# A fused attention, SwiGLU and layer-norm kernel: ScalarE's first tanh placed between two pairs of q copies

## The chip, the cores and the metric

The kernel runs on one core of a Trainium2 chip. The time is the device time of one execution in microseconds (us); lower is better. PE is TensorE, ACT is ScalarE, DVE is VectorE, POOL is GpSimd, and SP issues the DMAs.

## The reference, cut to what matters

There are 64 sequences of 64 tokens with 256 features. Everything is float32.

```
x = x + a_alpha * attention(gamma_a * rmsnorm(x) + beta_a)      # 16 heads of 16
x = x + f_alpha * (silu(h @ gate_w.T) * (h @ hidden_w.T) @ out_w.T + out_b)
                                                                # h = gamma_f * rmsnorm(x) + beta_f, 1024 hidden columns
y = (layernorm(x) * weight + bias + tanh(cond @ lin_w.T + lin_b)) * weight + bias
```

Each gamma, beta and alpha is a product of the sequence's condition vector (64 numbers) with a table. `silu(u)` is computed as `0.5 * u * (1 + tanh(u / 2))`, so each gate block needs one tanh on ACT.

## The kernel before, in words

The 64 sequences are cut into 8 groups (`GROUPS`) of 8 sequences, that is 512 tokens. The work is a software pipeline that is written out by hand as one instruction list for each engine: `head(g)` makes keys, values and queries of group g and finishes group g-2, and `main(g)` does the attention of group g together with the feed-forward part of the group before it, f = g-1. On each engine `head(1)`, `main(1)` and `head(2)` are written out, a hardware loop runs `main(i)`, `head(i + 1)` for i = 2 to 6, and `main(7)` and the end are written out again. So `head` with a group before it occurs seven times, for g = 1 to 7. Engines meet only through semaphores. Matrix products in float32 are done as three products of a high and a low part: six matmuls of 128x512 for one 128-column block with its 256 inputs.

The feed-forward part has 8 blocks c of 128 hidden columns. For each, PE makes a gate block and a hidden block (`gate_hidden`, L593, 12 matmuls). ACT applies tanh to the gate block in PSUM bank 2 and writes `act_t` (`tanh`, L778). DVE makes (tanh + 1) * gate (L1106), which frees bank 2, and then multiplies by half of the hidden block in bank 3 (L1110, which frees bank 3). ACT copies the result to `hs` as its high part (`hidden_hi`, L785), and POOL makes the low part (L1288). PE multiplies both with the output weights (`ffn_out`, L616). Bank 2 is the only gate bank in `main`, so the gate block c+1 waits until DVE's L1106 of block c is done (L580, semaphore `h_steps`).

For block 0, PE does four gate and four hidden matmuls first, then the last two of the gate and the last two of the hidden block, since those last ones need the low part that POOL makes of the normed input (`x2s`, L1273).

The change touches the place where `head(g)` hands over to `main(g)`. PE ends `head(g)` with the q projection (`q_proj`, L418) into banks 4 and 5. These two banks are read by two engines: DVE makes `qpar` (`q_out`, L1037, four instructions, first two of bank 4 and then two of bank 5), and ACT makes `qpair` (`pair_q`, L749, four instructions, first two of bank 5, h = 1, and then two of bank 4, h = 0). Each engine waits for the other's first pair before it goes on to the second (`qpair_ready`, `q_ready`), so that they do not read one bank together.

PE's `main(g)` goes on with `gate_hidden(f, 0)`, `scores_for_max(g, 0)`, `scores_for_max(g, 1)` (L478, eight matmuls each), `gate_hidden(f, 1)`, `ffn_out(f, 0)` and so on. `scores_for_max(g, 0)` writes banks 6 and 7. `scores_for_max(g, 1)` writes banks 4 and 5, where q lies, so it first waits for all four `qpar` and all four `qpair` copies:

```
                if n == 1 and later(g):
                    pe.wait_ge(q_ready, 4 * g + 4)
                    pe.wait_ge(qpair_ready, 4 * g + 4)
```

ACT's order before is `pair_q(g)` at the end of `head(g)`, then at the start of `main(g)` `feed(f, 0)`, which is `tanh(f, 0)` and `hidden_hi(f, 0)`, then two copies that place v (L763), then `feed(f, 1)`.

Of the kernel before, what the change touches and what calls it, by code (L numbers as in the profile page):

```python
# [88 lines left out]
def build(nc, x, condT, tabT, linT, linb, lnw, lnb, wqkT, wvT, woT, ghT, outT, outb_dram,  # L89
          consts, out):  # L90
    with ExitStack() as ctx:
# [124 lines left out]
        def later(g):  # L216

            return not isinstance(g, int) or g > 0
# [498 lines left out]
        def _(act):  # L717
            def cut_hi(n):
                act.wait_ge(ld_stage[n], 16)
                nc.scalar.activation(chunks[n][1], stage_view(n), ACT.Copy).then_inc(stage_hi, 1)  # L720
# [6 lines left out]
            def xs_split(g):  # L727
                act.wait_ge(xn_beta, g)
                nc.scalar.activation(xs[:, 0], xn[:, :, :], ACT.Copy).then_inc(xs_hi, 1)

            def k_out(g):

                act.wait_ge(k_mm, g + 1)
                for j in range(2):
                    nc.scalar.activation(kpair[:, :, j, :], banks[:, 4:6, :], ACT.Copy,  # L735
                                         scale=cst[:, C_PAIR + j:C_PAIR + j + 1]).then_inc(k_ready, 1)
                for e in range(2):
                    nc.scalar.activation(kpar[:, :, :, e, :], by_seq(banks[:, 4:6, :]), ACT.Copy,
                                         scale=cst[:, C_PAR + e:C_PAR + e + 1]).then_inc(k_ready, 1)

            def pair_q(g):

                base = 4 if later(g) else 0
                act.wait_ge(q_mm, g + 1)
                for h in (1, 0):
                    if h == 0:
                        act.wait_ge(q_ready, 4 * g + 2)
                    for j in range(2):
                        nc.scalar.activation(qpair[:, h, j, :], banks[:, base + h, :], ACT.Copy,  # L749
                                             scale=cst[:, C_PAIR + j:C_PAIR + j + 1]).then_inc(qpair_ready, 1)  # L750

            def keep_v(g):
                act.wait_ge(v_mm, g + 1)
                nc.scalar.activation(v_kept, banks[:, bank_of_v(g):bank_of_v(g) + 2, :].rearrange("p k n -> p (k n)"),
                                     ACT.Copy).then_inc(v_out, 1)
# [10 lines left out]
            def place_v_kept(g):  # L766
                act.wait_ge(v_out, g + 1)
                place_v(g, v_kept, True)

            def place_v_swapped(g):  # L770
                act.wait_ge(v_moved, 32 * g + 32)
                place_v(g, v_swapped, False)

            def tanh(f, c, base=2):
                act.wait_ge(gate_mm, CH * f + c + 1)
                if c >= 2 or later(f):
                    act.wait_ge(h_lo, CH * f + c - 1)
                nc.scalar.activation(act_t[:, c % 2, :], banks[:, base, :], ACT.Tanh, scale=0.5)\  # L778
                    .then_inc(tanh_ready, 1)

            def hidden_hi(f, c):
                act.wait_ge(h_steps, 2 * CH * f + 2 * c + 2)
                if c >= 2 or later(f):
                    act.wait_ge(out_mm, CH * f + c - 1)
                nc.scalar.activation(hs[:, c % 2, 0, :], act_t[:, c % 2, :], ACT.Copy).then_inc(h_hi, 1)  # L785

            def exp(g, n):
                base = bank_of_st(g, n)
                act.wait_ge(st_mm, 4 * g + n + 1)
                if n >= 2 or later(g):  # L790
                    act.wait_ge(o_mm, 2 * g + n // 2)
                b = 4 * (n % 2)
                nc.scalar.activation(pt[:, b:b + 4].rearrange("p b (a j) q -> p a b (j q)", a=2),  # L793
                                     banks[:, base:base + 2, :].rearrange("p a (b n) -> p a b n", b=4), ACT.Exp,
                                     scale=SCALE).then_inc(p_ready, 1)

            def o_split(g, h):
                act.wait_ge(o_steps, 4 * g + 2 * h + 2)
                nc.scalar.activation(os_[:, 0, h, :], work_c[:, 1, :], ACT.Copy).then_inc(o_hi, 1)  # L799

            def x2_split(g):
                for k in range(KD):
                    act.wait_ge(x2_beta, KD * g + k + 1)
                    nc.scalar.activation(x2s[:, 0, k], x2g[:, k, :], ACT.Copy).then_inc(x2s_hi, 1)

            def keep_x2(f):

                if later(f):
                    act.wait_ge(x3_steps, X3 * f)
                else:  # L810
                    act.wait_ge(stage_lo, len(chunks))
                nc.scalar.activation(x2c[:, :, :], x2[:, :, :], ACT.Copy).then_inc(x2_kept, 1)

            def scale_x3(f, tiles=range(TT)):

                act.wait_ge(ln_mean, f + 1)
                for t in tiles:
                    nc.scalar.activation(final[:, t, :], final[:, t, :], ACT.Identity,
                                         scale=nt1[:, 1, 1, t:t + 1], bias=mean_rs[:, t:t + 1])\
                        .then_inc(ln_scaled, 1)  # L820

            def feed(f, c, base=2):
                tanh(f, c, base)
                hidden_hi(f, c)

            def head(g):
                k_out(g)
                keep_v(g)
                place_v_kept(g)
                x2_split(g - 1)  # L830
                pair_q(g)

            def first():
                cut_hi(0)
                cut_hi(1)
                x0_split()
                cut_hi(2)
                k_out(0)
                pair_q(0)
                keep_v(0)  # L840
                act.wait_ge(zeroed, ZEROED)
                place_v_kept(0)
                act.wait_ge(setup_dve, SETUP_TANH)
                nc.scalar.activation(cvec, cvec, ACT.Tanh).then_inc(setup_act, 1)
                cut_hi(3)
                cut_hi(4)
                place_v_swapped(0)
                exp(0, 0)
                exp(0, 1)
                exp(0, 2)  # L850
                exp(0, 3)
                cut_hi(5)
                o_split(0, 0)
                cut_hi(6)
                cut_hi(7)
                o_split(0, 1)
                xs_split(1)

            def main(g, more=True, ln=True):
                f = g - 1  # L860

                feed(f, 0)
                place_v_swapped(g)
                for c in range(1, 4):
                    feed(f, c)
                    if c == 1:
                        if not later(f):
                            cut_hi(8)
                        keep_x2(f)
                exp(g, 0)  # L870
                exp(g, 1)
                tanh(f, 4)
                if ln:
                    scale_x3(g - 2)
                hidden_hi(f, 4)
                exp(g, 2)
                exp(g, 3)
                o_split(g, 0)
                tanh(f, 5)
                hidden_hi(f, 5)  # L880
                tanh(f, 6)
                o_split(g, 1)
                hidden_hi(f, 6)
                if more:
                    xs_split(g + 1)
                feed(f, 7, 2 if more else 4)

            first()
            head(1)
            main(1, ln=False)  # L890
            head(2)
            with act.Fori(2, GROUPS - 1) as i:
                main(i)
                head(i + 1)
            main(GROUPS - 1, more=False)
            x2_split(GROUPS - 1)
            for c in range(CH):
# [501 lines left out]
```

## Time and profile before

| | |
|---|---|
| median of 3 runs | 531.24 us (531.03 to 531.25) |
| the profiled execution's own time | 531.03 us |
| its span | 529.2 us |
| PE busy | 492.5 us (93%) |
| DVE busy | 393.0 us (74%) |
| ACT busy | 246.6 us (47%) |
| POOL busy | 241.5 us (46%) |
| PE's share of the chain that ended last | 78% |

The span is the time between the first and the last instruction in the trace; the execution's own time is 1.8 us more. The chain is found by going back from the last instruction, at each step to what released it. Times of single instructions are starts in us from the start of the span, and durations. Matmuls overlap one another, so that a group of matmuls ends later than the next one starts.

### The profile page before, as it was taken

How to read it: one execution, taken by the hardware profiler on the slowest of the kernel's cores; microseconds unless marked ns; L12 is line 12 of the kernel's file. 1: busy time of each engine (PE TensorE's matmuls, PEld its weight loads, DVE VectorE, ACT ScalarE, POOL GpSimd, SP SyncE). 2: the span in 40 equal slices, each digit the busy share in tenths (PEclk: the TensorE clock that was granted, in tenths of full speed). 3: DMA queues.
4: the chain of work that ended last, by engine and by line, in shares of the span. 5: the costliest groups of instructions: out<-in, count | busy, mean ns of one | idle time of the engine just before them, and what ended most of it. 6: DMA issues, size and time to landing. Idle time of an engine off the chain costs nothing.

```text
span 529.2 us, 11681 instructions
## 1 busy us (share of the span) xinstructions
PE 492.5 (93%) x4512; PEld 410.8 (78%) x4512; DVE 393.0 (74%) x792; ACT 246.6 (47%) x354; POOL 241.5 (46%) x165
## 2 busy tenths in 40 slices
PE   7874989999999999999999999999999999989990
PEld 4663867798788978798788978898888978876890
DVE  4787787678886788677886888777876886775636
ACT  2653464327453473537462574437462664322430
POOL 3343374354246443754256343663266341634452
PEclk9976999999999999999999999999999999998996
DMA  7481081003503070203402080204303060301021
GB/s 222 148 201 41 0 204 42 1 2 78 123 1 84 0 197 2 64 15 93 105 0 79 0 198 0 79 0 118 81 0 79 0 160 1 82 1 41 0 81 40
DMA packets 30650, 35.22 MB, mean 67 GB/s; under 512 B 1824, under 2 KB 28704, under 8 KB 30624
## 3 DMA queue, kind: packets, MB, share of 16 engines
q1 hardware_dynamic: 30624, 34.86, 25.4%
q8 instruction: 18, 0.29, 0.2%
q14 instruction: 8, 0.07, 0.1%
HBM read 26.27 MB, written 4.39 MB: 58 GB/s over the span
## 4 chain that ended last, share of the span: by engine, by line
PE 78%; DVE 9%; ACT 4%; POOL 3%; issue 2%; DMA 1%; SPq 1%; ACTq 0%; POOLq 0%; DVEq 0%
PE banks L593 30%; PE banks L616 17%; PE banks L418 7%; PE banks L514 5%; PE banks L543 4%; PE banks L448 3%; PE banks L529 3%; PE banks L534 2%; DMA final<-outb_in 1%; DVE work_c L1057 1%; PE banks L564 1%; PE banks L403 1%; DVE act_t L1106 1%; PE banks L518 1%; DVE qpar L1037 1%
## 5 line engine op out<-in xcount | busy, mean ns | idle before, releaser
L593 PE MATMUL banks<-x2s,gh 128*128 128x512 f32 x768 | 192.0, 398 | 6.3 <-DVE act_t L1106 4.5
L593 PEld LDWEIGHTS banks<-x2s,gh 128*128 128x128 f32 x768 | 140.1, 188 | 40.0 <-DVE act_t L1106 5.9
L1288 POOL TENSOR_TENSOR hs<-act_t,hs 128x512 fp32r<-128x512 f32 x64 | 83.4, 1304 | 142.5 <-ACT hs L785 142.5
L616 PE MATMUL banks<-wout,hs 128*128 128x256 f32 x768 | 105.0, 286 | 0.9 <-POOL hs L1288 0.8
L616 PEld LDWEIGHTS banks<-wout,hs 128*128 128x128 f32 x768 | 97.2, 188 | 6.0 <-POOL hs L1288 1.2
L1106 DVE SCALAR_TENSOR_TENSOR act_t<-act_t,banks 128x512 f32<-128x512 f32 x64 | 44.0, 688 | 55.8 <-ACT act_t L778 54.5
L785 ACT ACTIVATE hs<-act_t 128x512 fp32r<-128x512 f32 x64 | 40.3, 630 | 92.6 <-DVE act_t L1110 90.4
L778 ACT ACTIVATE act_t<-banks 128x512 f32<-128x512 f32 x64 | 38.2, 597 | 77.3 <-PE banks L593 76.0
L1057 DVE RECIPROCAL work_c<-banks 128x512 f32<-128x512 f32 x16 | 53.7, 3357 | 5.9 <-PE banks L529 5.9
L1110 DVE SCALAR_TENSOR_TENSOR act_t<-act_t,banks 128x512 f32<-128x512 f32 x64 | 44.0, 688 | 6.2 <-PE banks L593 0.6
L418 PE MATMUL banks<-xs,wqk 128*128 128x512 f32 x192 | 47.1, 394 | 0.0
L1043 DVE TENSOR_REDUCE smax<-banks 128x16 bf16<-128x1024 f32 x32 | 37.5, 1218 | 5.2 <-PE banks L478 5.2
L418 PEld LDWEIGHTS banks<-xs,wqk 128*128 128x128 f32 x192 | 35.1, 188 | 7.7 <-POOL xs L1259 0.3
L793 ACT ACTIVATE pt<-banks 128x1024 f32<-128x1024 f32 x32 | 32.0, 1020 | 16.6 <-PE banks L518 13.7
L514 PE MATMUL banks<-qpair,kpar 64*128 64x128 f32 x512 | 37.9, 289 | 0.4 <-DVE negmax L1049 0.4
L1263 POOL TENSOR_TENSOR os<-work_c,os 128x512 fp32r<-128x512 f32 x16 | 20.6, 1284 | 35.4 <-ACT os L799 35.4
L514 PEld LDWEIGHTS banks<-qpair,kpar 64*128 64x128 f32 x512 | 32.6, 195 | 3.9 <-issue 3.1
L1268 POOL TENSOR_TENSOR x2g<-x2g,tabs 128x512 f32<-128x512 f32 x16 | 16.8, 1069 | 40.0 <-DVE x2g L1099 40.0
L735 ACT ACTIVATE kpair<-banks,cst 128x1024 bf16<-128x1024 f32 x16 | 17.0, 1111 | 24.7 <-PE banks L418 24.7
L534 PEld LDWEIGHTS banks<-pt,vblk 128*32 128x32 f32 x1024 | 17.6, 114 | 10.2 <-issue 10.2
L1037 DVE TENSOR_SCALAR qpar<-banks,cst 128x512 bf16<-128x512 f32 x32 | 22.0, 744 | 3.7 <-PE banks L418 2.3
L448 PEld LDWEIGHTS banks<-wv,xs 128*128 128x128 f32 x192 | 24.1, 191 | 0.6
(123 smaller groups left out, 676.1 us busy)
## 6 DMA issues: line engine op xcount, KB each, us to landing
xtok<-x_in SPq DMA_DIRECT2D x8, 512.0 KB, 5.3
work_c<-xn SPq DMA_DIRECT2D x16, 256.0 KB, 3.6
row_aa<-rows_dram SPq DMA_DIRECT2D x16, 256.0 KB, 6.9
xres<-x_in SPq DMA_DIRECT2D x8, 512.0 KB, 7.4
row_af<-rows_dram SPq DMA_DIRECT2D x16, 256.0 KB, 7.1
shift<-rows_dram SPq DMA_DIRECT2D x16, 256.0 KB, 4.4
y<-final SPq DMA_DIRECT2D x7, 512.0 KB, 3.3
x2n<-wqkT_in SPq DMA_DIRECT2D x1, 512.0 KB, 5.3
```

Source lines behind the costliest of these rows:

```text
L418: last = mm(banks[:, base + m, :], wqk[:, a, k, c:c + P], xs[:, b, k, :], start=(n == 0), stop=(n == 5))
L448: last = mm(banks[:, base + t // 2, D * (t % 2):D * (t % 2) + D], xs[:, a, k, P * t:P * t + P], wv[:, b, k, :], start=(n == 0), stop=(n == 5))
L514: mm(region(i, half), kpar[r, h, b], qpair[r, h, :, L * b:L * b + L], start=(i == 0), stop=False)
L593: last = mm(banks[:, base + part, :], gh[:, a, k, w:w + P], x2s[:, b, k, :], start=(n == 0), stop=(n == 5))
L616: last = mm(banks[:, t // 2, D * (t % 2):D * (t % 2) + D], hs[:, c % 2, b, P * t:P * t + P], wout[:, a, c, :], start=False, stop=(c == CH ...
L778: nc.scalar.activation(act_t[:, c % 2, :], banks[:, base, :], ACT.Tanh, scale=0.5)\
L785: nc.scalar.activation(hs[:, c % 2, 0, :], act_t[:, c % 2, :], ACT.Copy).then_inc(h_hi, 1)
L1043: V.tensor_reduce(smax[:, :, 8 * n:8 * n + 8], banks[:, base:base + 2, :].rearrange("p a (x c) -> p a x c", c=L), AX.X, ALU.max).then_inc( ...
L1057: V.reciprocal(work_c[:, 0, :], banks[:, 7, :]).then_inc(o_steps, 1)
L1106: V.scalar_tensor_tensor(out=a, in0=a, scalar=1.0, in1=banks[:, base, :], op0=ALU.add, op1=ALU.mult).then_inc(h_steps, 1)
L1110: V.scalar_tensor_tensor(out=a, in0=a, scalar=0.5, in1=banks[:, base + 1, :], op0=ALU.mult, op1=ALU.mult).then_inc(h_steps, 1)
L1288: tt(hs[:, c % 2, 1, :], act_t[:, c % 2, :], hs[:, c % 2, 0, :].bitcast(F32), ALU.subtract)\
```

## The change

ACT's `pair_q` gets an argument for which of its two pairs it does. In `head(g)` the tanh of the gate block 0 of the group before (f = g-1) is issued between the pair of bank 5 and the pair of bank 4; `main(g)` then starts with `hidden_hi(f, 0)` alone. No instruction is added or removed on any engine but for some register and semaphore bookkeeping on ACT, and no DMA is touched.

```diff
-            def pair_q(g):
+            def pair_q(g, halves=(1, 0)):
 
                 base = 4 if later(g) else 0
                 act.wait_ge(q_mm, g + 1)
-                for h in (1, 0):
+                for h in halves:
                     if h == 0:
                         act.wait_ge(q_ready, 4 * g + 2)
                     for j in range(2):
...
                 x2_split(g - 1)
-                pair_q(g)
+                pair_q(g, (1,))
+                tanh(g - 1, 0)
+                pair_q(g, (0,))
...
             def main(g, more=True, ln=True):
                 f = g - 1
 
-                feed(f, 0)
+                hidden_hi(f, 0)
                 place_v_swapped(g)
```

On ACT, the end of the loop's body (`head(i + 1)`) and what comes behind it. L749 are the q copies, L778 is the tanh, L785 `hidden_hi`, L763 the copies of v; L892 (L894 in the changed kernel) is the loop's branch. Before:

```order
L749 ACTIVATE qpair<-banks,cst 128x512 [waits q_mm]
L749 ACTIVATE qpair<-banks,cst 128x512
L747 ISA
L749 ACTIVATE qpair<-banks,cst 128x512 [waits q_ready]
L749 ACTIVATE qpair<-banks,cst 128x512
L892 REGISTER_ALU
L892 COMPARE_AND_BRANCH
L778 ACTIVATE act_t<-banks 128x512 [waits h_lo,gate_mm]
L785 ACTIVATE hs<-act_t 128x512 [waits out_mm,h_steps]
```

Now:

```order
L749 ACTIVATE qpair<-banks,cst 128x512 [waits q_mm]
L749 ACTIVATE qpair<-banks,cst 128x512
L775 ISA
L777 REGISTER_ALU [waits gate_mm]
L778 ACTIVATE act_t<-banks 128x512 [waits h_lo]
L747 ISA [waits q_mm]
L749 ACTIVATE qpair<-banks,cst 128x512 [waits q_ready]
L749 ACTIVATE qpair<-banks,cst 128x512
L894 REGISTER_ALU
L894 COMPARE_AND_BRANCH
L785 ACTIVATE hs<-act_t 128x512 [waits out_mm,h_steps]
```

The tanh with its wait for the gate block has moved ahead of the last two q copies and of the loop's branch.

On PE, the rows of the same place, in the start of `main`; they are the same before and now. L593 first ends the blocks of c = 0, the two L478 rows with waits begin `scores_for_max(g, 0)` and `(g, 1)`, and the next L593 is the gate block of c = 1:

```order
L593 MATMUL banks<-x2s,gh 128x512 [waits x2s_lo] x2
L593 MATMUL banks<-x2s,gh 128x512 x2
L478 MATMUL banks<-kpair,qpar 128x128 [waits k_ready,q_ready,v_out]
L478 MATMUL banks<-kpair,qpar 128x128 x7
L478 MATMUL banks<-kpair,qpar 128x128 [waits qpair_ready,q_ready,max_ready]
L478 MATMUL banks<-kpair,qpar 128x128 x7
L593 MATMUL banks<-x2s,gh 128x512 [waits h_steps]
L593 MATMUL banks<-x2s,gh 128x512 x5
```

Nothing moved on PE; the order in which ACT reaches the two things that these rows wait for, `qpair_ready` and (through DVE) `h_steps`, is what the change turns round.

## Rows read from the trace of the kernel before

**Rows 1.** The page: busy time of each engine, and the chain's shares.
```profile
PE 492.5 (93%) x4512; PEld 410.8 (78%) x4512; DVE 393.0 (74%) x792; ACT 246.6 (47%) x354; POOL 241.5 (46%) x165
...
PE 78%; DVE 9%; ACT 4%; POOL 3%; issue 2%; DMA 1%; SPq 1%; ACTq 0%; POOLq 0%; DVEq 0%
```

**Rows 2.** PE's waits, 84.5 to 464 us: us in total, times, longest.
```profile
PE banks L593 <- DVE act_t L1106: 4.1, 7, 0.7
```

**Rows 3.** The chain in order of time, 302 to 325 us: start, us.
```profile
309.73 0.61 ACT act_t L778
...
310.36 0.70 DVE act_t L1106
311.06 0.04 issue
311.10 3.06 PE banks L593 x12
```

**Rows 4.** Timeline of PE: start, us, line, tiles, count, idle time before.
```profile
309.84 0.62 PE L478 MATMUL banks<-kpair,qpar 64*128 64x128 bf16 x16
311.10 3.06 PE L593 MATMUL banks<-x2s,gh 128*128 128x512 f32 x12 [0.64 <-DVE act_t L1106]
```

**Rows 5.** Timeline of POOL and ACT, groups 1 and 5: x2s and the tanh.
```profile
69.24 2.71 POOL L1273 TENSOR_TENSOR x2s<-x2g,x2s 128x512 fp32r<-128x512 f32 x2
...
72.54 0.60 ACT L778 ACTIVATE act_t<-banks 128x512 f32<-128x512 f32 x1 [0.28 <-PE banks L593]
...
307.57 1.31 POOL L1273 TENSOR_TENSOR x2s<-x2g,x2s 128x512 fp32r<-128x512 f32 x1
```

**Rows 6.** Timeline of ACT: q copies of group 5; a tanh with work behind it.
```profile
307.12 1.27 ACT L749 ACTIVATE qpair<-banks,cst 128x512 f32<-128x512 f32 x2 [0.36 <-PE banks L418]
308.57 1.27 ACT L749 ACTIVATE qpair<-banks,cst 128x512 f32<-128x512 f32 x2 [0.18 <-DVE qpar L1037]
...
285.71 0.60 ACT L778 ACTIVATE act_t<-banks 128x512 f32<-128x512 f32 x1 [3.47 <-PE banks L593]
286.20 0.62 ACT L799 ACTIVATE os<-work_c 128x512 fp32r<-128x512 f32 x1
```

**Rows 7.** Timeline of PE: 16 score matmuls with no wait, then L593.
```profile
315.98 0.62 PE L478 MATMUL banks<-kpair,qpar 64*128 64x128 bf16 x16
316.53 3.05 PE L593 MATMUL banks<-x2s,gh 128*128 128x512 f32 x12
```

**Rows 8.** Timeline of DVE, 307 to 316 us.
```profile
307.12 2.73 DVE L1037 TENSOR_SCALAR qpar<-banks,cst 128x512 bf16<-128x512 f32 x4 [0.16 <-PE banks L418]
...
311.68 2.35 DVE L1043 TENSOR_REDUCE smax<-banks 128x16 bf16<-128x1024 f32 x2
```

**Rows 9.** By stretches: stretch, length, busy of PE, PEld, DVE, ACT, POOL, then granted clock.
```profile
251.06:310.10 59.04, 58.38 (x566) 49.61 (x560) 45.98 (x91) 29.67 (x44) 28.48 (x19) 1.00 0.25 61
```

**Rows 10.** The chain in order of time, 70 to 86 us (group 1).
```profile
74.61 0.63 ACT hs L785
...
79.16 0.96 ACT wout L720
...
83.58 0.59 ACT act_t L778
```

**Rows 11.** PE's waits, 464 to 529 us.
```profile
PE banks L564 <- DVE x2n L1093: 2.1, 1, 2.1
```

**Rows 12.** Timeline of PE: an idle time in group 1.
```profile
68.91 0.47 PE L593 MATMUL banks<-x2s,gh 128*128 128x512 f32 x1 [0.93 <-ACT x2s L804]
```

**Rows 13.** Busy time by stretches; the granted clock is the third number from the end.
```profile
63.00:71.00 8.00, 6.31 (x30) 4.41 (x30) 7.32 (x13) 6.39 (x10) 6.48 (x5) 1.00 0.48 126
...
478.00:479.00 1.00, 1.00 (x6) 0.86 (x5) 0.68 (x2) 0.00 (x0) 0.00 (x0) 0.62 0.00 0
479.00:481.00 2.00, 2.00 (x6) 1.14 (x4) 1.97 (x4) 0.63 (x1) 1.91 (x2) 0.50 0.00 0
481.00:482.00 1.00, 0.80 (x2) 0.29 (x3) 1.00 (x1) 0.63 (x1) 1.00 (x2) 0.67 0.00 0
```

## The prediction

> **What bounds the kernel now.** I read the page first: PE is busy 93% of the span, and 78% of the chain that ended last is PE's [rows 1]. So only what makes PE wait, or lets it wait less, moves the time. Next I read PE's waits in the steady part, 84.5 to 464 us: one kind of wait is left there, seven times and 4.1 us in all, for DVE's L1106, which frees the gate bank [rows 2]. One of the seven lies in group 1's own chain, the other six are one for each handover from head to main, g = 2 to 7. The change aims at that wait, and it can win at most these six: about 6 x 0.64 = 3.8 us.
>
> Then I read one handover, g = 5, in the chain. It goes through ACT's last q copy, the tanh at 309.73, DVE's L1106 at 310.36, and PE's gate block 1 at 311.10 [rows 3]. On PE, the 16 score matmuls start at 309.84, and 0.64 us of idle time stand before 311.10 [rows 4]. One can state the handover as a rule: gate block 1 starts 311.10 - 309.73 = 1.37 us after the start of the tanh. In that path the tanh waits for two things, its turn behind four q copies, and its gate block. The last matmul of the gate block waits for POOL's second L1273. In group 1 the tanh had nothing ahead of it, and it started at 72.54, when that POOL work had ended at 69.24 + 2.71 = 71.95: 0.59 us behind it. In group 5 POOL ends at 307.57 + 1.31 = 308.88, so the gate block is ready for a tanh at 309.47 [rows 5]. The tanh really starts at 309.73, so the q copies hold it up by only **0.26 us**. That is all the change can give at this place.
>
> **The change, step by step** (group 5, as an example).
>
> 1. The first pair of q copies is not touched: 307.12 to 308.39 [rows 6]. ACT then stands at the tanh, whose gate block comes at 309.47, 1.1 us later. ACT is a queue in order, so the second pair, which could start at 308.57 before, now stands behind a wait.
>
> 2. The tanh starts at 309.47 in place of 309.73: a gain of 0.26. DVE's L1106 follows it as before, so `h_steps` would let gate block 1 start at 309.47 + 1.37 = 310.84.
>
> 3. The second pair starts behind the tanh. Where a tanh has ready work behind it, that work starts 286.20 - 285.71 = 0.49 us after the tanh's start [rows 6]. A pair of copies takes 1.27 us [rows 6]. The pair ends at 309.47 + 0.49 + 1.27 = 311.23, where it ended at 308.57 + 1.27 = 309.84 before: 1.39 us later.
>
> 4. Who waits for the pair? `scores_for_max(g, 1)` on PE, since it overwrites the q banks. It stands ahead of gate block 1 in PE's order. Before, the pair was complete at 309.84, when the first scores began, and cost nothing. Now PE runs the first eight score matmuls and stops. With 0.05 us from an ACT end to PE's start (I take the 0.04 us between DVE's end and PE in [rows 3] as nearest, and round), the second eight start at 311.28. Sixteen of them take 316.53 - 315.98 = 0.55 us until L593 starts [rows 7], so eight take 0.28. Gate block 1 starts at 311.56.
>
> 5. Sum for one handover: 311.56 against 311.10, **0.46 us later**. In terms of the tanh's start: before it was tanh + 1.37, now it is tanh + 0.49 + 1.27 + 0.05 + 0.28 = tanh + 2.09. The new path is 0.72 us longer and starts 0.26 us earlier. The changed kernel also has one register operation and one more semaphore instruction in ACT's queue around the tanh, with the wait on the register operation, and PE's row has three waits. I have no row for what these cost behind a release; I bound it between nothing and 0.2 us in one handover, five times the gap of 0.04 us that "issue" has between DVE's end and PE's start in the chain [rows 3]. I take 0.04, near the row: **0.50 us**, with ends 0.40 and 0.65.
>
> 6. What is hidden at no cost. DVE's q copies end at 307.12 + 2.73 = 309.85 as before [rows 8]; they need only ACT's first pair. DVE's own maxima: the first starts at 311.68 now and would start 0.26 earlier; the second needs the scores that end by about 311.7, and its turn comes only at 311.42 + 1.2 = 312.6. `hidden_hi(f, 0)` and all behind it on ACT come 0.26 us earlier, since the second pair ends at 311.23 and the copy is due at 309.47 + 2.07 = 311.54 (74.61 less 72.54 is 2.07 in group 1 [rows 5, 10]). The loop's branch falls into that gap. No DMA is issued otherwise; the move of v and the loads on SP's queue hang on events that the change doesn't move, or on PE's.
>
> 7. Does the later start get absorbed? One pass of the loop has 59.04 us with PE busy for 58.38 [rows 9]: what is left is the 0.64 us of this very wait. No other wait of PE stands in the pass, so nothing absorbs it, and what waits for PE shifts with it. Six handovers (g = 2 to 7) give 6 x 0.50 = **3.0 us**.
>
> 8. Group 1 is different. There the tanh waited for its gate block anyway, so the gain is 0, and PE comes 0.72 us later to gate block 1. But the chain does not go through PE behind it: it goes from that first tanh over ACT and DVE to ACT's cut of an output weight at 79.16, to POOL's work on it, and to the tanh of block 2 at 83.58 [rows 10]. None of these waits for the q copies or the second scores (ACT's q copies would end at 72.54 + 0.49 + 1.27 = 74.30, ahead of `hidden_hi` at 74.61). I take 0, with 0.72 as the upper end.
>
> 9. The end. After 464 us PE waits 2.1 us for DVE's norm [rows 11]; DVE hangs on PE there, so the shift goes through whole. Behind that wait the granted clock is at 0.62, 0.50 and 0.67 of 2.4 GHz for 478 to 482 us, that is at its level of 1.2 GHz for about 3.4 us [rows 13]. There it lies mostly over transposes and filling matmuls. If the same stretch falls a little later, it lies over gate matmuls, and costs up to half of 3.4, 1.7 us; if it falls earlier it can give little back, since what it slows now is mostly hidden behind DVE and POOL, and I allow 0.3. I take 0.
>
> 10. The clock in the handovers. PE's idle time there grows from 0.64 to about 1.1 us. In a pass with one such wait the granted clock is 1.00 [rows 9], and it is 1.00 in the stretch with an idle time of 0.93 us [rows 12, 13]; the fall at 478 us came behind 2.1 us [rows 11]. So I take the clock as full, and this step as 0. The Trainium skill (TensorE: Matmul & The Clock Gate, section "A second HAM failure mode: psum-queue depth-cycling") says that short idle times between groups of matmuls, repeated in each iteration, can make the clock swing between its two levels; by it the sum would be 544.4, and by the rows it stays as it is.
>
> Sum: 531.03 (the profiled execution) + 3.0 = 534.0; the median of the runs stands 0.21 above the profiled execution, so 531.24 + 3.0 = **534.2 us**, 0.6% slower.
>
> **The rivals.**
>
> *The clock falls in the longer wait* (step 10). If each handover were followed by a stretch like the one at the end, 3.4 us at 1.2 GHz [rows 13], matmuls would take twice as long in it, and each would cost 1.7 us more: 534.2 + 6 x 1.7 = 544.4. For it speaks only that 1.1 us lies above what the steady part shows, against it the clock of 1.00 at 0.93 us. Chance 0.04.
>
> *Faster.* The tanh is the last thing that PE's gate block 1 waits for, as before, and the q copies are in time. Then each handover gains 0.26: 531.24 - 6 x 0.26 = 529.7. It decides at the end of the second pair: `scores_for_max(g, 1)` must start by 310.84 - 0.28 = 310.56, so the pair must end by 310.5, and I have it at 311.23. It would need the tanh 0.72 us earlier, before POOL's low part is even made. Only if my reading of which wait guards the scores is wrong does this happen. Chance 0.03.
>
> *No difference.* The later start is absorbed behind the handover: 531.2. Against it is the pass without another wait of PE [rows 9]. The same result comes if ACT and PE overlap more than the rows say. Chance 0.04.
>
> *The slow clock at the end lands on gate matmuls* (step 9), or group 1 is not absorbed (step 8): 534.2 + 1.7 = 535.9. Chance 0.06.
>
> **How the numbers follow.** My forecast, the sum above, has 0.83, and 534.2 us is its value. Its own ends are 6 x 0.40 = 2.4 and 6 x 0.65 = 3.9, with 0.2 of measurement and 0.3 for the end: 533.2 to 535.2. The range reaches on to 535.6 for most of the case at the end and of group 1. It leaves out the clock, the gain and no difference, 0.11 together, and something of the rest. A measurement of this kernel can tell 0.2%, about 1.1 us, from no change. Faster by more than that: 0.03 (only the second rival, and 529.7 is 1.5 below). Within it: 0.04. Slower: 0.93.
>
> **What would show it right or wrong.** PE's waits should have a new kind, L478 <- ACT qpair L749, six or seven times and about 1 us each, and L593 <- DVE L1106 should be gone from the handovers. The tanh should start about 0.6 us behind POOL's L1273, with two q copies behind it. One pass should take 59.5 us at clock 1.00. L593 <- L1106 still there with passes of 58.8 us would make me wrong, and so would a clock under 1.00 in a pass, or a pass of 59.5 us with a total that didn't grow by six times that.

## The result, and the profile after

The changed kernel takes 534.47 us (median of 6 runs, 533.87 to 535.32) against 531.13 us for the kernel before in the same comparison (6 runs, 530.00 to 531.27). The ratio is 1.0075, with a 95% interval of 1.0059 to 1.0092 (the two medians alone give 1.0063): it is slower by about 0.75%, and the forecast of 534.2 us, slower, within 533.2 to 535.6, holds. The profiled execution took 534.05 us with a span of 532.3 us, 3.0 us more than before (532.25 against 529.23).

The page of the changed kernel, busy time of each engine and shares of the chain:

```profile
PE 491.3 (92%) x4512; PEld 410.8 (77%) x4512; DVE 392.1 (74%) x792; ACT 246.6 (46%) x354; POOL 241.4 (45%) x165
...
PE 83%; DVE 7%; ACT 4%; POOL 3%; issue 2%; ACTq 0%; POOLq 0%; DVEq 0%
```

No engine has more work than in [rows 1]. PE has less busy time in a longer span, so it waits more. What it waits for in the steady part, 90 to 463 us (us in total, times, longest):

```profile
PE banks L478 <- ACT qpair L749: 7.3, 6, 1.2
```

This stands in the place of [rows 2], of which 4.0 us in six waits lie in this stretch: the wait for DVE's product is gone, and a new one has come, 1.8 times as long, of the second set of score matmuls for ACT's last q copy. Its longest is 1.2 us against 0.7. The same handover as in [rows 4, 6], g = 5, on PE (start, us, idle time before):

```profile
307.04 2.95 PE L593 MATMUL banks<-x2s,gh 128*128 128x512 f32 x12
309.92 0.40 PE L478 MATMUL banks<-kpair,qpar 64*128 64x128 bf16 x8
311.55 0.40 PE L478 MATMUL banks<-kpair,qpar 64*128 64x128 bf16 x8 [1.23 <-ACT qpair L749]
311.88 0.50 PE L593 MATMUL banks<-x2s,gh 128*128 128x512 f32 x1
```

and on ACT:

```profile
307.24 1.27 ACT L749 ACTIVATE qpair<-banks,cst 128x512 f32<-128x512 f32 x2 [0.37 <-PE banks L418]
309.65 0.60 ACT L778 ACTIVATE act_t<-banks 128x512 f32<-128x512 f32 x1 [1.14 <-PE banks L593]
310.14 1.26 ACT L749 ACTIVATE qpair<-banks,cst 128x512 f32<-128x512 f32 x2
311.80 0.63 ACT L785 ACTIVATE hs<-act_t 128x512 fp32r<-128x512 f32 x1 [0.40 <-DVE act_t L1112]
```

The 16 score matmuls, one block before, are cut in two. ACT stands idle for 1.14 us at the tanh while two copies that could run wait behind it, and PE then waits for those copies. Gate block 1 starts 311.88 - 307.04 = 4.84 us behind block 0, where it was 311.10 - 306.92 = 4.18. Of POOL, the second low part of the normed input ends where it did, seen from PE:

```profile
306.43 2.55 POOL L1275 TENSOR_TENSOR x2s<-x2g,x2s 128x512 fp32r<-128x512 f32 x2 [0.39 <-ACT x2s L804]
```

One pass of the loop (stretch, length, busy time of PE, PEld, DVE, ACT, POOL, granted clock), before and after. The row of before is a neighbour of [rows 9]; here each stretch goes from block 0 of one group to that of the next:

```profile
247.89:306.92 59.03, 58.37 (x559) 49.62 (x558) 45.98 (x92) 29.66 (x43) 28.46 (x20) 1.00 0.25 62
```

The changed kernel:

```profile
247.34:307.04 59.70, 58.47 (x560) 49.65 (x559) 45.96 (x92) 29.66 (x43) 28.44 (x20) 1.00 0.24 61
```

The clock is full in both, and PE is busy for 0.10 us more, so 0.57 of the 0.67 us are waiting. The 16 score matmuls, cut in two, make PE busy for 2 x 0.40 us where they made it busy for 0.62 in one piece. The whole execution divides, by the starts of block 0 of each group in the two traces, like this (us):

| part | before | changed | difference |
|---|---|---|---|
| start to block 0 of group 2 | 129.82 | 128.01 | -1.81 |
| five passes, to block 0 of group 7 | 295.17 | 298.43 | +3.26 |
| to block 0 of the last feed-forward part | 55.86 | 57.14 | +1.28 |
| the rest | 48.38 | 48.67 | +0.29 |

The six handovers lie in the second and third part: 3.26 there, and some 0.66 of the 1.28. The rest is the setup and the end, where the granted clock falls and rises at other places in every execution. The start is 1.81 us shorter here (13.7 us of it at the lower level of the clock, against 17.1), and the end is 0.62 and 0.29 us longer: at 478.5 us the clock is low already under the transposes, which in the kernel before ran mostly ahead of the fall in [rows 13].

The stretch at the lower clock in the kernel before and in the changed kernel (the clock is the third number from the end):

```profile
478.20:481.60 3.40, 3.40 (x9) 1.94 (x7) 3.25 (x4) 1.06 (x2) 2.51 (x3) 0.51 0.00 0
...
478.50:485.30 6.80, 5.85 (x17) 4.36 (x18) 5.06 (x10) 1.26 (x2) 3.49 (x4) 0.50 0.00 0
```

The transposes of the changed kernel, on PE:

```profile
479.25 1.97 PE L564 MATMUL banks<-cst,x2n 128*128 128x128 f32 x8 [2.11 <-DVE x2n L1095]
```

The eight transposes took 1.24 us before.

### The profile page after: what moved, and what is told of

It reads as the page before. It is cut to its first block, busy times and chain, and to the rows that moved or that the text cites. A ratio compares the mean times of both kernels' runs of the same rounds, so it can differ in the third digit from the quotient of the medians.

```text
span 532.3 us, 11683 instructions
## 1 busy us (share of the span) xinstructions
PE 491.3 (92%) x4512; PEld 410.8 (77%) x4512; DVE 392.1 (74%) x792; ACT 246.6 (46%) x354; POOL 241.4 (45%) x165
## 4 chain that ended last, share of the span: by engine, by line
PE 83%; DVE 7%; ACT 4%; POOL 3%; issue 2%; ACTq 0%; POOLq 0%; DVEq 0%
PE banks L593 33%; PE banks L616 17%; PE banks L418 7%; PE banks L514 5%; PE banks L543 4%; PE banks L448 3%; PE banks L529 3%; PE banks L534 2%; ACT qpair L749 2%; PE banks L375 2%; PE banks L564 1%; PE banks L403 1%; DVE work_c L1059 1%; PE banks L518 1%; PE banks L478 1%
## 5 line engine op out<-in xcount | busy, mean ns | idle before, releaser
L593 PE MATMUL banks<-x2s,gh 128*128 128x512 f32 x768 | 192.2, 399 | 0.8 <-ACT x2s L804 0.6
L593 PEld LDWEIGHTS banks<-x2s,gh 128*128 128x128 f32 x768 | 140.4, 189 | 33.9 <-ACT x2s L804 2.0
L616 PE MATMUL banks<-wout,hs 128*128 128x256 f32 x768 | 104.8, 286 | 0.4 <-POOL hs L1290 0.3
L616 PEld LDWEIGHTS banks<-wout,hs 128*128 128x128 f32 x768 | 97.2, 188 | 5.3 <-POOL hs L1290 0.5
L778 ACT ACTIVATE act_t<-banks 128x512 f32<-128x512 f32 x64 | 38.2, 597 | 90.3 <-PE banks L593 89.0
L785 ACT ACTIVATE hs<-act_t 128x512 fp32r<-128x512 f32 x64 | 40.3, 630 | 85.0 <-DVE act_t L1112 81.2
L1265 POOL TENSOR_TENSOR os<-work_c,os 128x512 fp32r<-128x512 f32 x16 | 20.5, 1284 | 35.5 <-ACT os L799 35.5
```

The costliest lines, as they stand in the source:

```text
L593: last = mm(banks[:, base + part, :], gh[:, a, k, w:w + P], x2s[:, b, k, :], start=(n == 0), stop=(n == 5))
L616: last = mm(banks[:, t // 2, D * (t % 2):D * (t % 2) + D], hs[:, c % 2, b, P * t:P * t + P], wout[:, a, c, :], start=False, stop=(c == CH ...
```

## The experiments

On the chips of the experiments the single runs of the kernel before spread over 529.4 to 537.3 us, since the setup and the end differ from run to run. So I read the mechanism from the traces, in two numbers that hold still: the start of gate block 1 behind block 0 (**the handover**), and the **pass**, from block 0 of one group to that of the next (the passes inside the loop agree within 0.03 us in each trace, the first in it being up to 0.1 shorter). The table has the handovers of the loop. The first of the six, that of group 2, comes out of `head(2)`, which is written out: it is up to 0.1 shorter where the tanh waits for its gate block (4.76 in the changed kernel). The six give the expected difference in the total.

| kernel | handover | pass | ratio to before, interval |
|---|---|---|---|
| before | 4.18 | 59.03 | |
| changed | 4.84 | 59.70 | 1.0075 [1.0059, 1.0092] |
| e1, tanh behind four copies | 4.17 | 59.03 | 0.9992 [0.9963, 1.0021] |
| e2, tanh behind three copies | 4.26 | 59.12 | 0.9981 [0.9946, 1.0017] |
| e3, changed ACT, scores behind gate block 1 | 3.99 | 59.60 | 1.0052 [1.0017, 1.0087] |
| e4, old ACT, scores behind gate block 1 | 4.17 | 59.70 | 1.0060 [1.0021, 1.0099] |
| e5, three copies, both preparations | 3.87 | 58.72 | 0.9981 [0.9948, 1.0014] |
| e6, four copies, both preparations | 4.17 | 59.03 | one run |
| e7, three copies, ACT's preparation | 4.26 | 59.13 | one run |
| e8, three copies, PE's preparation | 4.26 | 59.11 | one run |
| e9, change in group 1 alone | 4.17 | 59.04 | one run |
| e10, the changed kernel again | 4.84 | 59.69 | 1.0074 [1.0036, 1.0112] |
| e11, e5 again | 3.87 | 58.72 | 0.9961 [0.9930, 0.9992] |

My theory: PE's second scores wait for the last q copy, whose end is set by the tanh's own wait. The rivals: the new place of the tanh in ACT's queue costs (its register operation, the branch), or the tanh's own time is what PE feels.

Each ratio is to runs of the kernel before on the same chip. All kernels compute the whole reference.

**e1: the place without the order.**

```diff
-                pair_q(g, (1,))
-                tanh(g - 1, 0)
-                pair_q(g, (0,))
+                pair_q(g)
+                tanh(g - 1, 0)
```

> The tanh is issued at the end of ACT's head, behind all four q copies and ahead of the loop's branch: the change's place in the program without its order. Theory (PE waits for the last q copies, whose end the tanh sets): the order on ACT is the old one, PE waits 0.64 us a handover for DVE's L1108 as before, one pass takes 59.03 us, the time is 531.1 us, ratio 1.000. Rival (the tanh's wait, its register operation and the branch behind it cost the time, whatever the order): near 534.5 us, a pass near 59.7 us.

PE's waits in e1, 90 to 463 us:

```profile
PE banks L593 <- DVE act_t L1107: 4.0, 6, 0.7
```

PE's only wait from 90 to 463 us is the old one, with the old size, and the pass is the old one. The place of the tanh in the program, ahead of the branch, costs nothing. The rival falls as a cause of the 0.66 us.

**e2: three copies, then the tanh.**

```diff
-                pair_q(g, (1,))
-                tanh(g - 1, 0)
-                pair_q(g, (0,))
+                pair_q(g, ((1, 0), (1, 1), (0, 0)))
+                tanh(g - 1, 0)
+                pair_q(g, ((0, 1),))
```

> Three q copies, then the tanh, then the fourth. Theory, with what the changed kernel's trace measured (tanh 2.61 us behind the start of PE's block 0, next work on ACT 0.49 later, one copy 0.68, PE starts 0.14 behind it, eight score matmuls 0.33): gate block 1 starts 2.61 + 0.49 + 0.68 + 0.14 + 0.33 = 4.25 us behind block 0, against 4.18 before and 4.84 in the changed kernel. Six handovers cost 0.4 us: 531.5 us, ratio 1.001; PE's wait L478 <- ACT L749 is about 0.65 us each. Rival (it is not the copies' end that counts, but that any copy stands behind the tanh's wait, or the tanh's own place): near 534.5 us. Other rival (the tanh 0.20 earlier is what counts for PE): 529.9 us.

PE's waits in e2, the same stretch:

```profile
PE banks L478 <- ACT qpair L749: 3.8, 6, 0.7
```

The wait is for the copy again, 0.63 us a time, and the handover is 4.26, the 4.25 of the sum. One copy fewer behind the tanh takes 0.58 us away, the distance from one copy to the next (a pair of 1.27 us in [rows 6] less 0.69 for one). This decides between "any copy behind the tanh costs" and "the end of the last copy counts": it is the end. The total, 0.9981, does not resolve the 0.4 us.

**e3 and e4: nobody waits for the copies at once.** On PE and DVE, in both:

```diff
                 scores_for_max(g, 0)
-                scores_for_max(g, 1)
                 if fed:
                     gate_hidden(f, 1)
+                scores_for_max(g, 1)
...
                 max_over_keys(g, 0)
-                max_over_keys(g, 1)
                 feed(f, 1)
+                max_over_keys(g, 1)
                 max_over_keys(g, 2)
```

e3 has ACT's changed order, e4 the old one.

> The changed ACT order, but PE does scores_for_max(g, 1) behind gate_hidden(f, 1), and DVE takes its maximum behind feed(f, 1). Nobody that PE needs at once waits for the late q copies. Theory: gate block 1 starts at tanh + 1.37 = 2.61 + 1.37 = 3.98 us behind block 0, and the eight score matmuls of 0.28 us come elsewhere: 4.26 in all against 4.18 before and 4.84 in the changed kernel; 531.6 us, ratio 1.001, no wait L478 <- ACT L749 is left. Rival (the later scores only move the wait: DVE's maxima are now late and PE waits for max_ready ahead of the next scores): a new wait L478 <- DVE smax of up to 1 us, 533 us and over. Rival (the cost lies in ACT's own queue): stays near 534.5 us.

> The PE and DVE order of the run before with ACT's old order, to part the two. Theory: gate block 1 starts at 2.81 + 1.37 = 4.18 us as before, but the 0.28 us of score matmuls no longer lie in the wait: 4.46 in all, six times 0.28 = 1.7 us: 532.8 us, ratio 1.003. So on this PE order the moved tanh is worth 0.20 us a handover, a gain of 1.2 us, where on the old one it costs 4. Rival (DVE's later maxima cost here too): over 533.5 us. Rival (reordering costs nothing by itself): 531.1.

PE in e3, one handover:

```profile
312.25 3.06 PE L593 MATMUL banks<-x2s,gh 128*128 128x512 f32 x12 [0.70 <-DVE act_t L1109]
315.24 0.40 PE L478 MATMUL banks<-kpair,qpar 64*128 64x128 bf16 x8
315.57 0.73 PE L609 MATMUL banks<-outb,ones 128*128 128x512 f32 x2
316.13 1.59 PE L616 MATMUL banks<-wout,hs 128*128 128x256 f32 x12
317.65 0.84 PE L478 MATMUL banks<-kpair,qpar 64*128 64x128 bf16 x16
```

and DVE:

```profile
316.21 0.69 DVE L1113 SCALAR_TENSOR_TENSOR act_t<-act_t,banks 128x512 f32<-128x512 f32 x1
316.82 3.63 DVE L1046 TENSOR_REDUCE smax<-banks 128x16 bf16<-128x1024 f32 x3
```

With the score matmuls out of the way the wait for the copies is gone, and gate block 1 starts at 3.99, the tanh + 1.37 of the prediction, 0.19 earlier than before. That is the gain the tanh's place can give, and e4, where it starts at 4.17, shows that it comes from the tanh. But the rest did not come out as I expected: the pass is 59.60 in e3, where the sum gives 59.11, and 59.70 in e4, where it gives 59.31. Of the 0.19 us at gate block 1 only 0.10 are left in the pass, and the totals (1.0052 and 1.0060) do not part the two kernels. The rival on DVE's maxima was right for a part of it. The second maximum now waits behind both products of block 1 and starts at 316.82. The last eight score matmuls, which overwrite its banks, are released by it: the 16 take 0.84 us and not 0.62, and the next gate block starts at 10.16 us behind block 0, where it is 9.61 before. The 0.55 us are made up like this: -0.19 up to gate block 1; +0.42 from there to L609, the eight score matmuls that moved there and what it takes to start them; +0.10 from L609 to L616 (0.56 against 0.46), for which I have no cause; and +0.22 for this wait. In e4 the loss is 0.67: 0.00, 0.42, 0.11 and 0.15 at the same places, less 0.01 from L616 to the score matmuls. So this order loses on PE more than it gives.

**e5 to e8: an earlier gate block.** In e2 the tanh still waits for its gate block, and the copy for the tanh. Two preparations make the gate block ready earlier. ACT's, in `head`:

```diff
-                place_v_kept(g)
-                x2_split(g - 1)
+                act.wait_ge(v_out, g + 1)
+                place_v(g, v_kept, True, (0,))
+                x2_split(g - 1, (0,))
+                place_v(g, v_kept, True, (1,))
+                x2_split(g - 1, (1,))
```

PE's, in `gate_hidden`, for block 0:

```diff
-                    steps.sort(key=lambda step: step[1] >= 4)
+                    steps = [(0, n) for n in range(4)] + [(1, 0), (1, 1), (0, 4), (0, 5)] + \
+                        [(1, n) for n in range(2, 6)]
```

e5 has both and e2's order of tanh and copies, e6 both and the old order, e7 ACT's alone and e8 PE's alone, both with e2's order.

> Three q copies, tanh, fourth copy; with it the tanh's gate block made ready earlier in two ways: ACT does the high parts of the normed input between its two v placements, so that POOL's second low part ends 0.38 us earlier (1.58 us behind the start of block 0 in place of 1.96), and PE does the last two gate matmuls of block 0 behind two hidden matmuls in place of four. Theory: the last gate matmul starts at 1.65 and ends at 2.05, the tanh could start at 2.16 and is held by the third copy to 2.23; the fourth copy ends at 2.23 + 0.49 + 0.68 = 3.40, gate block 1 starts at 3.40 + 0.14 + 0.33 = 3.87 against 4.18 before: a pass of 58.72 us, six handovers give 1.9 us: ratio 0.9965. Rival (the v placement that is now later, or PE's reordering, costs what is won): a pass of 59.0 us or more.

> The same two preparations with ACT's old order, four copies and then the tanh. Theory: the gate block is ready at 2.16, but the tanh starts only behind the copies at 2.81, so gate block 1 starts at 4.18 and a pass takes 59.03 us as before. Rival (the gate block's end alone is what counts): a pass of 58.6 us.

> Three copies, tanh, fourth copy, and ACT's mixed order, but PE's old order of block 0. Theory: the last gate matmul starts at 2.10 for PE's own pace, so POOL's 0.38 us are worth nothing: gate block 1 at 4.26, a pass of 59.13 us as with three copies alone. Rival (POOL's low part is the limit): 0.3 us less.

> Three copies, tanh, fourth copy, and PE's new order of block 0, but ACT's old order. Theory: PE stands at the last gate matmul until POOL is done at 1.96, starts it at 2.02, the tanh starts at 2.53, gate block 1 at 2.53 + 0.49 + 0.68 + 0.14 + 0.33 = 4.17; a pass of 59.03 us. Rival (the wait in the middle of block 0 adds to the handover): 59.4 us.

The timeline of ACT and PE in one handover of e5, block 0 being at 305.17:

```profile
306.81 0.69 ACT L750 ACTIVATE qpair<-banks,cst 128x512 f32<-128x512 f32 x1 [0.18 <-DVE qpar L1043]
307.40 0.59 ACT L779 ACTIVATE act_t<-banks 128x512 f32<-128x512 f32 x1
307.88 0.69 ACT L750 ACTIVATE qpair<-banks,cst 128x512 f32<-128x512 f32 x1
...
308.71 0.40 PE L478 MATMUL banks<-kpair,qpar 64*128 64x128 bf16 x8 [0.23 <-ACT qpair L750]
...
309.04 3.06 PE L594 MATMUL banks<-x2s,gh 128*128 128x512 f32 x12
```

One pass, in e11, the same kernel once more:

```profile
249.09:307.81 58.72, 58.52 (x559) 49.64 (x558) 45.90 (x92) 29.77 (x43) 28.43 (x20) 1.00 0.24 62
```

The tanh starts at 2.23 and gate block 1 at 3.87, each as summed; the pass of 58.72 stands in e5 and in e11, and PE's waiting in it is down to 0.2 us. e6 gives 59.03 and e7 59.13, as expected: with four copies ahead the tanh is held by the copies, and with PE's old order its own pace ends the gate block, whatever POOL does. e8 was expected at 59.03 and gave 59.11, with the handover at 4.26 where 4.17 was due. PE and ACT in e8, block 0 starting at 305.83:

```profile
305.83 1.79 PE L594 MATMUL banks<-x2s,gh 128*128 128x512 f32 x7
307.83 1.41 PE L594 MATMUL banks<-x2s,gh 128*128 128x512 f32 x5 [0.21 <-POOL x2s L1276]
309.18 0.40 PE L478 MATMUL banks<-kpair,qpar 64*128 64x128 bf16 x8
309.76 0.40 PE L478 MATMUL banks<-kpair,qpar 64*128 64x128 bf16 x8 [0.19 <-ACT qpair L750]
...
308.44 0.60 ACT L779 ACTIVATE act_t<-banks 128x512 f32<-128x512 f32 x1 [0.28 <-PE banks L594]
```

PE stands for 0.21 us in the middle of block 0, and the block ends later, but that is not what costs: the second scores still wait 0.19 us for the copy behind it. The miss lies in the tanh, which starts at 2.61 and not at 2.53. The last gate matmul, the one at 307.83, starts at 2.00, as summed, but it is the first behind a wait and takes 0.50 us in the trace, where the sum has some 0.40 (gate block 1 of the changed kernel also begins with one of 0.50 behind its wait). So it ends at 2.50, just where that of e2 ends (2.09 + 0.41), and the tanh, the copy and the handover are those of e2.

So each preparation alone gives nothing, and both together give 0.31 us a handover.

**e9: group 1 alone.** All groups but the first have the old order.

```diff
+                if isinstance(g, int) and g == 1:
                     pair_q(g, (1,))
                     tanh(g - 1, 0)
                     pair_q(g, (0,))
+                else:
+                    pair_q(g)
...
+                if not (isinstance(g, int) and g == 1):
+                    tanh(f, 0)
                 hidden_hi(f, 0)
```

> The change in group 1's head alone; groups 2 to 7 have the old order. Theory: from the first tanh of group 1 to block 0 of group 2 it takes 57.40 us, as in the changed kernel, against 57.28 before (0.12 us more, since the second product of block 1 waits for its late hidden block), and all passes take 59.03 us. Rival (group 1 absorbs it whole, and the 0.12 us came from elsewhere): 57.28 us. In the total nothing that a measurement could tell.

From group 1's first tanh to block 0 of group 2 it took 57.37 us, with the loop's passes at 59.02 to 59.05. The changed kernel has 57.40 and e10 57.39; the kernel before has 57.28, and all others lie at 57.25 to 57.31. Group 1 costs about 0.1 us, too little for any total to show.

**e10 and e11: the two ends once more, on one chip.**

> The changed kernel as it is, once more, beside the kernel before on the same chip: passes of 59.69 us against 59.03, and with six handovers of 0.66 us 4.0 us in all, ratio 1.0075. If the total differs from that by more than the start and the end of the program do, something outside the handovers is touched.

> The kernel with three copies ahead of the tanh and both preparations, once more, for its interval: passes of 58.72 us, six handovers give 1.9 us, ratio 0.9965 to the kernel before and 0.989 to the changed kernel.

One pass of e10:

```profile
252.37:312.06 59.69, 58.46 (x560) 49.63 (x558) 45.98 (x92) 29.63 (x43) 28.44 (x20) 1.00 0.25 62
```

The changed kernel has the pass of its first trace to 0.01 us, and the ratio 1.0074. Five handovers of 0.66, the one of group 2 with 0.59 and group 1's 0.1 are 4.0 us, for which 1.0075 is due. The version with both preparations has 0.9961, interval 0.9930 to 0.9992, where 6 x 0.31 = 1.9 us is 0.9965. Its medians are 531.73 us in e5 and 532.14 us in e11, against 532.95 and 534.85 us for the kernel before in the same comparisons and 538.66 us for the changed kernel in e10. It beats both kernels; against the one before this rests on a small difference in the totals, whose first comparison alone had no clear sign, and on the two traces, where it is plain.

## Why the prediction was right

*What bounds the kernel, and what the change can win.* Right in the number, wrong in one reading behind it. The only wait of PE in the steady part was the one the change aims at, and what the tanh's place holds up is small: 0.26 us was forecast, 2.81 - 2.61 = 0.20 measured (the tanh behind the start of block 0), 0.19 at gate block 1 in e3. The reading is that the last gate matmul waits for POOL's second low part. So it is in group 1 of the kernel before, where that matmul starts at 72.01 us, 0.05 behind POOL's end. In the loop it is the tenth of twelve that follow one another without idle time, 0.23 us apart: in group 5 it starts at 309.02, 0.14 us after POOL had ended at 308.88, and PE's own pace sets it. e7 shows the same: POOL ends 0.38 us earlier there and the tanh starts where it did. The matmul ends at 309.44, so a tanh could start at 309.47, the forecast's number; that the gap of group 1 gave the same number here is luck. In the changed kernel's loop the tanh starts 309.65 - 308.98 = 0.67 us behind POOL's end.

*Who waits for the moved copies* (steps 3 and 4). Right, and this was the whole case. The pair ends at tanh + 0.49 + 1.27 as summed, and PE's second scores wait for it. e1, e2 and e3 show it from three sides: behind all copies nothing changes, with one copy behind the tanh the loss shrinks to 0.08, and with nobody waiting gate block 1 comes early.

*The size of one handover* (steps 4 and 5). It was undersized: 0.50 us forecast, 0.66 measured, just above the upper end of 0.65. The terms: 0.06 for the tanh's later start; PE starts 0.14 us behind the last copy and not 0.05, 0.09 more; the eight score matmuls with their wait take 0.33 and not 0.28, 0.05 more. With the 0.46 of the sum this is 0.66. The chain of the changed kernel in order of time shows the second of these (start, us):

```profile
310.16 1.25 ACT qpair L749 x2
311.41 0.14 issue
311.55 0.40 PE banks L478 x8
```

Step 5 had 0.04 for the unseen cost of the extra operations and waits, inside bounds of 0 and 0.2; the three terms together are 0.20. So the bound held and the choice near its low end did not. The traces show what the terms are.

The first is the register operation that has the tanh's wait for its gate block in the loop (L777). It takes 0.035 us and starts 0.03 us behind the end of the gate block, and the tanh starts 0.08 us behind it. In `head(2)`, which is written out, the tanh has this wait itself. There it starts at 130.54 - 128.01 = 2.53 us behind block 0, not at 2.61, and that handover loses 0.59 us, not 0.66:

```profile
130.54 0.60 ACT L778 ACTIVATE act_t<-banks 128x512 f32<-128x512 f32 x1 [1.07 <-PE banks L593]
```

The second is an operation in PE's queue that has the wait for `qpair_ready` (L470, 0.05 us). It starts at 311.44, 0.04 us behind the copy's end, the first weight load stands at 311.52 and its matmul at 311.55. Gate block 1 has its wait on its own weight load and matmul and starts 0.04 us behind DVE's product. No experiment took the operation out. The third is that eight score matmuls by themselves take 0.33 us, also in e3, where no wait stands before them, and not half of what 16 take.

*What is hidden* (step 6). Right. ACT's `hidden_hi` comes in time, at 4.76 us behind block 0 (311.80 less 307.04), where it was 4.88 before, and DVE's maxima start at 311.61, 4.57 behind block 0 against 4.76. Both are earlier by less than the 0.26 us of the forecast, and nothing waits for them.

*No absorption* (step 7). Right. A pass grew by 0.66 us, all of what the handover grew by, and PE's busy time by 0.1. The six handovers are 3.9 us (five times 0.66 and once 0.59) against the 3.0 of the forecast, and 4.0 with group 1. The measured ratios of 1.0075 and 1.0074 are 4.0 us; the difference of the two medians, 3.3 us, lies between, since start and end differ from run to run. So it is partly luck that the median lies within 0.3 us of 534.2: with 4.0 us on the 531.13 of the kernel before it would be 535.1, in the range still, but near its upper end.

*Group 1* (step 8). I took 0 and it was 0.1. The chain over ACT and DVE does hold, but the second product of block 1 waits for a hidden block that PE begins later: ACT then waits 1.59 us for the product where it waited 1.47.

```profile
76.72 0.63 ACT L785 ACTIVATE hs<-act_t 128x512 fp32r<-128x512 f32 x1 [1.59 <-DVE act_t L1112]
```

*The end* (step 9). The slow clock did move over other work in this trace, and cost 0.9 us, inside the allowance of 1.7. The total there is no longer than in other traces: the last part takes 48.67 and 50.00 us in the changed kernel's two traces and 49.95 in e1's, with the old order. But whether the change has a part in where the clock falls stays open. The stretch at the lower clock near PE's last long wait is 6.8 us long in both traces of the changed kernel and 3.4 us in each of the eleven others, e3 with the changed order on ACT among them. In e10:

```profile
485.70:492.50 6.80, 6.42 (x15) 4.16 (x14) 3.37 (x4) 1.26 (x2) 4.51 (x4) 0.50 0.29 72
```

*The rivals.* The clock stayed at 1.00 through all passes with idle times of 1.23 us (step 10), so the rule of the Trainium skill on clocks that swing with short idle times (TensorE: Matmul & The Clock Gate, "A second HAM failure mode: psum-queue depth-cycling") did not take hold at this length. The faster rival asked for the copies by 310.5, and they came at 311.4 (in a trace in which block 0 is 0.12 us later). Its mechanism is real, as e5 shows, once the copies and the gate block are both in time.

## What to carry to other kernels

Work that waits for nothing, put behind an operation that waits for another engine, takes on that wait: ask for each thing moved back by a wait who reads it, and where that reader stands in its own engine's order. Here the path over the tanh became 0.20 us shorter, but the path over the copies, which had nothing to say before, now ends 0.86 us behind it, since it leads to work that stands first in PE's queue: 0.66 us lost. Measure a handover by the two paths into it and move only as much as levels them: three of four copies ahead of the tanh, with the tanh's input made ready earlier, was better than either two or four. Look also at which operation has the wait. Here a release cost 0.04 us where the waiting instruction had it itself, 0.11 where a register operation ahead of the tanh had it, and 0.14 where an operation ahead of PE's weight load had it; 0.05 for all was too little.

## What the runs showed that I had not expected

The time from the start to block 0 of group 2 was 128.0 to 135.4 us in 13 traces, though all of them run almost the same instructions there, and from the start of the last feed-forward part to the end 48.4 to 50.0. In the start the granted clock is at its lower level for 13.7 us in five traces (the changed kernel among them; 128.0 to 129.6 us), 17.1 in four (the kernel before among them; 129.8 to 131.6), 20.5 in two (e9 and e10; 132.3 and 133.1) and 23.9 in two (e6 and e7; 133.3 and 135.4), at other places in most. In e7 PE also waited 3.1 us for a load that it didn't wait for in the trace of the kernel before:

```profile
PE banks L390 <- DMA final<-outb_in: 3.1, 1, 3.1
```

So a change of 1 us in the steady part can't be seen in a few totals of this kernel, while its passes show it to 0.02 us.
